# Graph layer 2 on one core: every fourth tile as a dense 32-bit product instead of gathered rows

## What is computed

```python
h = jnp.maximum(_layernorm(x, axis=-1), 0.0)
x = x + _L0_gnn_ref(h, adj, ...)          # layer 1
h = jnp.maximum(_layernorm(x, axis=-1), 0.0)
x = x + jnp.matmul(adj, h @ W.T + b)      # layer 2
```

## Time and profile before

| | us |
|---|---|
| median of 3 runs | 1441.94 (1440.53 to 1447.99) |
| profiled execution, its time | 1447.69 |
| profiled execution, its span | 1446.2 |
| layer 1, first to last instruction | 0 to about 1026 |
| layer 2 and checks | about 1026 to 1446.2 |

### The profile page before, as it was taken

How to read it: one execution, slowest core, us unless ns; L and a number is a source line. 1 busy time by engine, 2 the same in 40 slices (tenths; PEclk the granted TensorE clock), 3 DMA queues, 4 the chain that set the end, 5 groups by cost and what they waited for, 6 DMA issues and landing times.

```text
span 1446.2 us, 16194 instructions
## 1 busy us (share of the span) xinstructions
PE 839.7 (58%) x4509; PEld 592.8 (41%) x4555; DVE 1076.1 (74%) x3642; ACT 686.5 (47%) x834; POOL 813.6 (56%) x818
## 2 busy tenths in 40 slices
PE   5457757765776677667756776676334444333343
PEld 4224434443544344345534444355233333333333
DVE  7475888989889889898898898966455555565554
ACT  6736456556466466565664665623222333332232
POOL 6435644554455445544553455442477777777774
PEclk9776888988889899878887898878555555555555
DMA  9998998888888988988889889711467666666763
GB/s 372 249 365 368 343 353 327 322 317 323 331 308 309 371 312 322 338 330 305 327 317 342 300 325 333 260 33 28 155 237 236 219 231 221 227 227 238 237 232 110
DMA packets 72866, 401.19 MB, mean 277 GB/s; under 512 B 15169, under 2 KB 41026, under 8 KB 52290
## 3 DMA queue, kind: packets, MB, share of 16 engines
q1 hardware_dynamic: 51138, 357.03, 64.5%
q0 software_dynamic: 20480, 42.48, 12.6%
q10 hardware_dynamic: 1152, 0.59, 0.1%
HBM read 387.35 MB, written 12.68 MB: 277 GB/s over the span
## 4 chain that ended last, share of the span: by engine, by line
DVE 38%; PE 31%; issue 20%; POOL 4%; ACT 3%; DMA 2%; SPq 1%; DVEq 0%; ACTq 0%
PE ACC L1179 10%; DVE Y L670 9%; PE ACC L1057 9%; DVE H L794 5%; DVE KS L678 4%; DVE H L927 4%; PE ACC L1085 4%; PE GP L1121 2%; PE GP L1124 2%; POOL H L409 2%; POOL H L457 1%; DVE KR L683 1%; DVE WG L857 1%; ACT H L503 1%; DMA X<-in_adj_dram 1%
## 5 line engine op out<-in xcount | busy, mean ns | idle before, releaser
L409 POOL DMA_INDIRECT H<-projected_rows,IDX x320 | 393.4, 1229 | 169.5 <-issue 87.8
L457 POOL DMA_INDIRECT H<-layer_rows,IDX x320 | 307.1, 960 | 104.9 <-issue 104.9
L503 ACT ACTIVATE H<-X 128x4096 uint8<-128x4096 uint32 x96 | 346.5, 3609 | 16.4 <-DMA X<-in_adj_dram 14.5
L1179 PE MATMUL ACC<-H 128*128 128x128 f32 x640 | 157.9, 434 | 254.5 <-issue 197.0
L1057 PE MATMUL ACC<-Y,DW 128*128 128x512 fp8e4 x768 | 239.6, 469 | 96.5 <-DVE Y L670 50.7
L1179 PEld LDWEIGHTS ACC<-H 128*128 128x128 f32 x640 | 141.2, 329 | 271.2 <-issue 234.3
L619 ACT ACTIVATE H<-X 128x4096 uint8<-128x4096 uint32 x32 | 115.7, 3617 | 284.2 <-DMA X<-in_adj_dram 284.2
L670 DVE TENSOR_SCALAR Y<-X 128x4096 fp8e4<-128x4096 f32 x96 | 222.5, 2322 | 18.4 <-DMA X<-in_adj_dram 18.4
L1057 PEld LDWEIGHTS ACC<-Y,DW 128*128 128x128 bf16 x768 | 82.2, 115 | 208.5 <-issue 59.0
L935 DVE TENSOR_TENSOR H<-ACC,WG 128x128 f32<-128x128 f32 x64 | 18.7, 292 | 185.7 <-PE ACC L1179 185.7
L941 DVE TENSOR_SCALAR_CACHE_REDUCE Y<-X 128x4096 fp8e4<-128x4096 f32 x32 | 141.0, 4408 | 0.0
(11 more groups left out here) (186 smaller groups left out, 1553.4 us busy)
## 6 DMA issues: line engine op xcount, KB each, us to landing
X<-in_adj_dram SPq DMA_DIRECT2D x160, 2048.0 KB, 10.4
H<-projected_rows,IDX POOLq DMA_INDIRECT x320
H<-layer_rows,IDX POOLq DMA_INDIRECT x320, 3.6
projected_rows<-WG SPq DMA_DIRECT2D x16, 262.0 KB, 9.0
H<-in_xb_dram SPq DMA_DIRECT2D x8, 512.0 KB, 8.5
R<-in_xb_dram SPq DMA_DIRECT2D x32, 128.0 KB, 9.2
layer_rows<-GT SPq DMA_DIRECT2D x32, 128.0 KB, 10.4
out_dram<-H SPq DMA_DIRECT2D x32, 128.0 KB, 1.9
```

The lines of the kernel that those rows point to most:

```text
L409: nc.gpsimd.indirect_dma_start(GB[q % 3][:, e, :], None, tab_d, bass.IndirectOffsetOnAxis(ap=IDX[:, 2 * KT5 * q + e:2 * KT5 * q + e + 1], ...
L457: nc.gpsimd.indirect_dma_start(GR[t % 6][:, e, :], None, g_d, bass.IndirectOffsetOnAxis(ap=IDX[:, KT5 * t + e:KT5 * t + e + 1], axis=0)).t ...
L503: nc.scalar.activation(J8, Xu[h % 4], ACT.Sign, accum_out=NZ[:, h:h + 1]).then_inc(a_nz, 1)
L1179: ins = nc.tensor.matmul(bank[t % 4][:, 0:F], SU[t % 4][:, e, :], GR[t % 6][:, e, :], start=(e == 0), stop=(e == KT5 - 1))
```

## The change

Layer 2 of the 16 late tiles no longer gathers. Instead PE multiplies the whole 128 x 8192 block of `adj` with all 8192 rows of `g`: 64 products of 128 x 128 x 128 in 32 bits per late tile (`dense_sums`). For that
- the host passes `adjt`, the late tiles' blocks transposed, so that they can be the stationary operand;
- SP loads all of `layer_1_rows` (4 MB) into `X[2]` and `X[3]` (`rows_again`, called `GX`), after the last `g_store` has landed; the late halves then alternate between `X[0]` and `X[1]` only, and a load waits, besides both counts, for the product that read the buffer (`n_pe2`);
- POOL, DVE and PE do the gathers, one-hots and products of L457, L927 and L1179 for the other 48 tiles only (`gathered`);
- the order is by groups: group g has the first two gathered tiles of the four, then the late tile of group g-1, then the third gathered tile (group 16 is late tile 63 alone);
- `OT` is now a ring of four single tiles, stored one by one; the n-th finished tile waits for the store of the (n-4)-th;
- SP's list for group g is: late loads 2g and 2g+1, then the stores of group g-1;
- `own_rows` leaves out the late tiles, whose diagonal is in the dense product. ACT's count writes to `Y`, DVE's to `J8`.

The core of the diff (SP, DVE, PE):

```diff
+        def group_of(g):
+            first = [t for t in gathered if t // LATE == g]
+            own = [late[g - 1]] if g > 0 else []
+            return first[:2] + own + first[2:]
+
+        finished = [t for g in range(GROUPS_N + 1) for t in group_of(g)]
...
                 def late_load(k):
...
+                    if k < 2:
+                        n = place([h for h in seen if h % 4 == k][-1])
+                        sp.wait_ge(d_y, n + 1)
+                        sp.wait_ge(a_nz, n + 1)
+                    else:
+                        sp.wait_ge(a_nz, len(seen) + k - 1)
+                        sp.wait_ge(d_on, k - 1)
+                        sp.wait_ge(n_pe2, k - 1)
+                    sp.dma_start(X[k % 2][:, :], adjt[k // 2, :, (k % 2) * HALF:(k % 2 + 1) * HALF]).then_inc(x_in[k % 2], 16)
+
+                def rows_again(c):
...
+                    sp.dma_start(GX[c // 4][:, c % 4 * 8:c % 4 * 8 + 8, :], g_t[:, 8 * c:8 * c + 8, :]).then_inc(
+                        rows_in[c], 16)
+
+                def store(t):
+                    n = finished.index(t)
+                    sp.wait_ge(d_out, n + 1)
+                    sp.dma_start(out[:, t, :], OT[n % 4]).then_inc(q_out[n % 4], 16)
+
+                for k in range(2):
+                    late_load(k)
+                for c in range(8):
+                    rows_again(c)
+                for g in range(GROUPS_N + 1):
+                    if 0 < g < GROUPS_N:
+                        late_load(2 * g)
+                        late_load(2 * g + 1)
+                    if g > 0:
+                        for t in group_of(g - 1):
+                            store(t)
+                for t in group_of(GROUPS_N):
+                    store(t)
...
                 def finish(t):
...
+                    n = finished.index(t)
+                    if n > 3:
+                        dve.wait_ge(q_out[n % 4], n // 4 * 16)
...
+                def row_sums(t):
+                    j = gathered.index(t)
+                    pe.wait_ge(d_su, j + 1)
+                    pe.wait_ge(g_e[j % 6], layer_1_pairs(j % 6) * 32 * KT5 + (j // 6 + 1) * 16 * KT5)
+                    if j > 3:
+                        pe.wait_ge(d_out, finished.index(gathered[j - 4]) + 1)
...
+                def dense_sums(m):
+                    if m == 0:
+                        for c in range(8):
+                            pe.wait_ge(rows_in[c], (NS // 4 + 2) * 16 if c < 4 else 32)
+                    if m > 1:
+                        pe.wait_ge(d_out, finished.index(late[m - 2]) + 1)
+                    for d in range(2):
+                        k = 2 * m + d
+                        pe.wait_ge(x_in[k % 2], (NT // 2 + k // 2 + 1) * 16)
+                        for b in range(NT // 2):
+                            ins = nc.tensor.matmul(GP[:, m % 2 * 512:m % 2 * 512 + F], X[k % 2][:, b * P:(b + 1) * P],
+                                                   GX[d][:, b, :], start=(d == 0 and b == 0),
+                                                   stop=(d == 1 and b == NT // 2 - 1))
+                        ins.then_inc(n_pe2, 1)
...
+                for j in range(3):
+                    unweighted(j)
+                for g in range(GROUPS_N + 1):
+                    for t in group_of(g):
+                        if t in late:
+                            if g < GROUPS_N:
+                                late_ones(2 * g)
+                                late_ones(2 * g + 1)
+                            else:
+                                tally()
+                        elif gathered.index(t) + 3 < len(gathered):
+                            unweighted(gathered.index(t) + 3)
...
+                        finish(t)
```

More of the change, by code:

```diff
@@ L54, with graph_layers @@
 AX = mybir.AxisListType
-def graph_layers(nc, xb, adj, w, wt, a, w_ih, w_hh, wiht, whht, b_ih, b_hh, w1, w1t, b1, out):
+def graph_layers(nc, xb, adj, adjt, w, wt, a, w_ih, w_hh, wiht, whht, b_ih, b_hh, w1, w1t, b1, out):
     outer = ExitStack()
@@ L63, in graph_layers @@
         redo = outer.enter_context(nc.sbuf_tensor("redo", [1, 1], mybir.dt.int32))
-        q_out = [sem(f"q_out{b}") for b in range(2)]
-        edge_lists(nc, sem, q_out, redo, xb, adj, w, wt, a, wiht, whht, b_ih, b_hh, w1t, b1, out)
+        q_out = [sem(f"q_out{b}") for b in range(4)]
+        edge_lists(nc, sem, q_out, redo, xb, adj, adjt, w, wt, a, wiht, whht, b_ih, b_hh, w1t, b1, out)
         needed = nc.values_load(redo[0:1, 0:1], min_val=0, max_val=1)
@@ L220, in edge_lists @@
         w_in, b_in, wt_in = sem("w_in"), sem("b_in"), sem("wt_in")
-        p_x = [sem(f"p_x{q}") for q in range(8)]
+        rows_in = [sem(f"rows_in{q}") for q in range(8)]
         p_id, p_one, p_con, p_wa, p_ab = sem("p_id"), sem("p_one"), sem("p_con"), sem("p_wa"), sem("p_ab")
@@ L241, in edge_lists @@
         g_out = [sem(f"g_out{b}") for b in range(2)]
-        a_nz, d_on = sem("a_nz"), sem("d_on")
-        g_r = [sem(f"g_r{b}") for b in range(6)]
+        a_nz, d_on, n_pe2 = sem("a_nz"), sem("d_on"), sem("n_pe2")
         d_su, l_pe, d_out = sem("d_su"), sem("l_pe"), sem("d_out")
@@ L257, in place, with layer_1_pairs @@
             return seen.index(h) if h in seen else None
+        def layer_1_pairs(b):
+            return len([q for q in range(NS) if q % 3 == b])
+        GROUPS_N = NT // LATE
+        gathered = [t for t in range(NT) if t not in late]
+        def group_of(g):
[3 more added lines that the diff above has]
+        finished = [t for g in range(GROUPS_N + 1) for t in group_of(g)]
         def side(h):
@@ L326, in late_load @@
+                def rows_again(c):
+                    if c == 0:
+                        for u in range(2):
+                            sp.wait_ge(g_out[u], NS // 2 * 16)
                         sp.wait_ge(c_half, 2 * NT)
                         sp.wait_ge(g_dx, NT)
-                        sp.wait_ge(d_y, len(seen))
                         sp.wait_ge(a_nz, len(seen))
-                    else:
-                        sp.wait_ge(a_nz, len(seen) + k - 3)
-                        sp.wait_ge(d_on, k - 3)
@@ L333, in late_load @@
[L333 to L344, removed]
@@ L615, in _, with late_map @@
                         nonzeros(4 * n + 3)
[L616 to L619, removed]
+                def late_map(k):
+                    h = unseen[k]
+                    act.wait_ge(x_in[k % 2], (NT // 2 + k // 2 + 1) * 16)
+                    if k == 0:
+                        act.wait_ge(c_half, 2 * NT)
+                        act.wait_ge(g_dx, NT)
+                    nc.scalar.activation(Y[k % 2][:, :], Xu[k % 2], ACT.Sign, accum_out=NZ[:, h:h + 1],
+                                         saturate=False).then_inc(a_nz, 1)
+                late_map(0)
+                late_map(1)
+                for k in range(2, len(unseen)):
+                    late_map(k)
             @block.vector
@@ L854, in own_rows @@
                     dve.wait_ge(ag_pe, q + 1)
-                    for u in range(2):
-                        t = 2 * q + u
+                    for t in [t for t in (2 * q, 2 * q + 1) if t not in late]:
+                        u = t % 2
                         ins = nc.vector.scalar_tensor_tensor(XG[:, t, :], GT[q % 2][:, u * F:(u + 1) * F], DG[:, t:t + 1],
```

108 lines of the change are left out of this document (54 added, 54 removed).

## The result

| | before | after |
|---|---|---|
| median, us (lowest to highest) | 1442.95 (1440.53 to 1447.99) | 1483.4 (1478.02 to 1487.59) |
| profiled execution, its time | 1447.69 | 1487.59 |
| its span | 1446.2 | 1485.8 |
| mean granted clock | 0.741 | 0.837 |

Four runs each; the ratio of the changed kernel to the one before is 1.0274, interval 1.0227 to 1.032: 2.7% slower. The prediction had 1496 us, 3.7% slower, in a range of 1462 to 1535.

What follows compares the result with a forecast made beforehand. POOL's gathers bounded layer 2; afterwards store waits would. First late tile to 1080.1, second to 1098.3, 13 rounds 378.3, last 16.9, tail 8.6, layer 1 less 3: span 1499.9, 53.7 longer; 1441.94 + 53.7 = 1496 us, range 1462 to 1535.

Steps and rivals of the forecast that it cites:

- What bounded the kernel before: Layer 2: POOL's gathers at 1.263 us each, 6.3 us a tile, 404 us for 64 tiles.
- The mechanism of the round: Layer 2: store, `finish`, one-hots chained after each late product; TensorE idle 8.7 us, then low clock; 29.1 us a round.
- The store lands with the load: SP's queue in layer 2: a store issued behind a 2 MB load takes 9.6 us, landing at 9.7.
- two rules of the Trainium skill: DMA rings: descriptors start in order but later ones may finish first; completion counts land behind all earlier writes of that engine.
- my allowance for the load that is still coming in: Store landing in a round: something added because load 2g, issued at about -7, still comes in until about +2.
- my one figure: Layer 2: each of 13 rounds takes 29.1 us, 378.3 in all.
- slower landings: Rival, layer 2 loads beside gather bursts: landing at 12.5, 3 us more in each of 13 rounds, 1535 us; 5%.
- The rival with 0.08: Late products: a long stream at 0.08 us a record saves 4.1 us a late tile, 14 times; about 1440 us; 2%.
- The rival "store not held": Layer 2: store lands 1.9 us after issue, rounds of 19.6 us, 9.5 less, 13 times; 1372 us; 7%.
- layer 1: I take 3: Layer 1: 16 of 64 instructions of L857 go; a quarter of its chain share is 3.6 us, taken as 3.
- the last late product: End of layer 2: no wait for one-hots, but its second half waits for its load; 16.9 us.
- the tail: From the last product to the end of the span: 8.6 us, as before.

Runs made afterwards that it cites:

- the list with the stores between: Changed kernel with the four stores of group g-1 placed between late load 2g and late load 2g+1: 1376.52 us, ratio 0.9535.
- the halved load: Changed kernel with late load 2g+1 cut into two of 1 MB, the stores between them: 1439.45 us, ratio 0.9955.
- the ring of eight: Changed kernel with eight output tiles instead of four, SP's list unchanged, DVE's counts writing to a free fp8 buffer: 1358.88 us, again 1356.74.

## Why the prediction was right, and where not

- **What bounded the kernel before, and that it would not bound it after:** right. With the wait gone a gather again takes 1.27 us and POOL has only its own pace as a limit.
- **The mechanism of the round:** right, step for step, in the 12 rounds behind the first. No store before the end of the late product; `finish` in the ring of four behind it; one-hots behind `finish`; TensorE idle with two gathered tiles done; low clock in the tile after the pause and at the start of the late product.
- **The store lands with the load:** right, and seen three times, in the two landings 0.35 us apart in the changed kernel, in the list with the stores between (0.47 us apart, behind the earlier load), and with the halved load. That the order in the one queue is the reason holds for a part at most: issued from ACT's queue, the store lands 2.4 us earlier in the mean, 7.2 against 9.6. The prediction names two rules of the Trainium skill, "DMA: Bandwidth & Descriptors" (Queues, rings and completion order). What these rows time is when a DMA's completion count releases an engine, and by the same section of the Trainium skill that count lands behind all earlier writes of the same DMA engine. The rows agree with it: in all 13 rounds of the changed kernel the store's completion comes 0.3 to 0.7 us behind that of the load ahead of it, in none before it.
- **The sizes in the round:** in the round shown, landing at 8.5 us after the late product instead of 9.7 and the gathered tile's start at 10.0 instead of 11.3; the gathered tile 2.3 as predicted and the late product 15.2 instead of 15.5. For such a round my allowance for the load that is still coming in was too large; that it landed when the other went out, the rows show (landed 1206.97, issued about 1206.5).
- **The mean of the rounds was partly luck.** Over 13 rounds, from the end of the second late product (1084.20) to that of the fifteenth (1458.88), it is 28.8 against 29.1, and the landing 9.6 against 9.7. But nine rounds were 1.3 to 2.1 us shorter than my one figure, and the first two were 5.1 and 3.4 us longer, where I had put 0.8 for the load that DVE's counts hold back; slower landings stood only among the rivals. The two errors largely cancel.
- **A long stream of products:** 128 records in 14.46 us are 0.113 each, just the 0.112 of the earlier trace rows. The rival with 0.08 fell.
- **The rival "store not held":** it did not come true, but its price can be compared. Its rounds would be 9.5 us shorter, and the time 1372. In the ring of eight, where nobody waits for a store, the rounds are 19.2 us against 28.8, 9.6 shorter, and the time is 1358.9. With the stores between the loads a short wait is left, and it is 21.1 us and 1376.5. The price of the wait was right, and it is more than the whole of the loss.
- **The step that failed** is the last term of the sum, "layer 1: I take 3". I took it from the line's average share of the chain; in layer 1 DVE is busy for 742.7 of 860 us (100 to 960 us of the kernel before), and the profile of the changed kernel has layer 1 13.6 us shorter. Leaving the 16 instructions out by themselves gave some 11 us of time in two kernels, and no difference in the median of the changed kernel.
- **The end:** the last late product took 15.4 us with the tile before it instead of 16.9, since its load landed within 7.6 us (ACT starts on it at 1466.54, the issue was at 1458.97). What follows took 11.5 us instead of 8.6: DVE's last two counts stand behind the last wait on a store (1466.72), so they end at 1476, after TensorE, and the tally starts at 1476.41. I had taken the tail over from the kernel before and not asked what the change puts ahead of the tally in DVE's list.

The sum for the span: 53.7 predicted, 39.6 measured. Layer 1 makes -10.6 of the difference, the rounds and the start -4.9, the last product -1.5, the tail +2.9. Between the medians it is 54 predicted and 40.5 measured.

## What to carry to other kernels

Before a list of DMAs in one queue is put in a new order, ask of every small transfer what stands ahead of it and who waits for its landing: behind a load of 2 MB it landed with the load here, and a queue of its own for the stores brought 1483 us down to 1451 only. Where the wait can't be moved, a deeper ring can take its price away: four more buffers of 64 KB were worth 8% here (1483.4 to 1358.9 us), where the change without them had lost 2.7%. And on an engine that is close to full, an instruction left out may be worth more than its duration, so try it alone. When a mean agrees with a forecast, look at the single rounds: here nine shorter and four longer ones made it up.

## What the runs showed that I had not expected

- A 64 KB store issued right behind a 2 MB load in the same queue lands with it (0.35 and 0.47 us behind it), behind a 1 MB load after 4.9 us in the median, and in another queue at the same moment after 8.1 in the median (5.8 for the first store of the round shown). With the last load already landed, twice the size took 1.9 us.
- With the loads behind the stores, the stores held back the loads: 1407.8 us against 1376.5 with the stores between the two loads.
- 16 instructions of DVE of 0.35 us were worth 11.4 us of 1368 in one kernel, some 11 in another, and nothing that the median shows in a third.
- In the ring of eight TensorE ran 32-bit products of 128 x 128 x 128 for 100 us with 95% busy time and a granted clock of 0.97, where layer 2 of the kernel before, gathered tiles alone, shows 0.50.
